# A third PSUM bank for the ring of turns and projections, taken from the score maxima

## The reference

```
# block 1: attention with a modulated norm, no mask
xn   = rms_norm(x, g_norm) * (1 + scale(cond)) + shift(cond)
q,k,v = split(xn @ W_qkv);  q = rms_norm(q, g_q); k = rms_norm(k, g_k)   # per head
a    = softmax(q k^T / sqrt(32)) v
x1   = a + a @ W_out

# block 2: attention with a latent, rotary halves and a causal mask, then experts
n    = rmsnorm(x1, ln1)
kv_d, q_d = n @ kv_d_w, n @ q_d_w                     # 128 wide
k = [kv_d @ k_u_w | rope(n @ rope_k_w)];  q = [q_d @ q_u_w | rope(q_d @ rope_q_w)]
v = kv_d @ v_u_w
h = x1 + softmax(causal(q k^T / sqrt(32))) v @ o_w
m = rmsnorm(h, ln2)
out = x + h + expert_shared(m) + sum over the top 2 of 7 routed experts(m)
```

## Time and profile before

| | |
|---|---|
| median of 3 runs | 1290.48 us |
| the profiled execution | 1290.86 us |
| its span, first to last instruction | 1289.1 us |
| TensorE busy | 1169.7 us (91%) |
| VectorE busy | 744.4 us (58%) |
| ScalarE busy | 572.3 us (44%) |
| GpSimd busy | 290.7 us (23%) |
| mean granted TensorE clock | 0.97 of full speed |
| chain that ended last, by engine | PE 77%, DVE 8%, DMA 5%, ACT 4% |

### The profile page before, as it was taken

One profiled execution on the slowest core, in us unless ns is written; L12 is line 12 of the kernel. 1 busy time (PEld: TensorE's weight loads), 2 busy tenths in 40 slices (PEclk: granted clock), 3 DMA queues, 4 the chain that ended last, 5 costly groups with the idle time before them and its releaser, 6 DMA issues.

```text
span 1289.1 us, 18670 instructions
## 1 busy us (share of the span) xinstructions
PE 1169.7 (91%) x6059; PEld 825.7 (64%) x6059; DVE 744.4 (58%) x1807; ACT 572.3 (44%) x1248; POOL 290.7 (23%) x244
## 2 busy tenths in 40 slices
PE   5979999999999889999999989989999999999970
PEld 5745555665566446557767757766657888888850
DVE  6565675477545856666565575566364774444433
ACT  3324464345443555455465454455264753222210
POOL 1313122100210031001011200200124464555530
PEclk9979999999999999999999999999899999999995
DMA  7064243125311732352284264265357744555559
GB/s 255 33 180 131 65 136 112 50 86 184 99 50 58 225 107 57 99 189 88 88 259 149 86 234 122 84 201 176 86 186 232 262 152 105 109 108 113 115 134 331
DMA packets 88127, 178.42 MB, mean 138 GB/s; under 512 B 12609, under 2 KB 23265, under 8 KB 86497
## 3 DMA queue, kind: packets, MB, share of 16 engines
q1 hardware_dynamic: 79216, 156.90, 37.4%
q0 software_dynamic: 8512, 19.93, 8.2%
q10 hardware_dynamic: 304, 0.40, 0.2%
HBM read 110.86 MB, written 65.27 MB: 137 GB/s over the span
## 4 chain that ended last, share of the span: by engine, by line
PE 77%; DVE 8%; DMA 5%; ACT 4%; issue 3%; SPq 1%; POOL 0%; DVEq 0%; ACTq 0%; POOLq 0%
PE psum L862 14%; PE psum L681 9%; PE psum L682 8%; PE psum L683 8%; PE psum L846 6%; PE psum L825 6%; PE psum L690 4%; PE psum L940 4%; PE psum L942 4%; PE psum L941 4%; PE psum L967 2%; PE psum L969 2%; PE psum L968 2%; PE psum L909 2%; PE psum L772 2%
## 5 line engine op out<-in xcount | busy, mean ns | idle before, releaser
L1174 ACT ACTIVATE probs<-psum 128x512 f32<-128x512 f32 (+3 forms) x512 | 257.3, 517 | 231.5 <-PE psum L849 120.6
L825 PE MATMUL psum<-stack 96*128 96x512 f32 (+3 forms) x512 | 210.2, 416 | 8.6 <-DMA stack<-split_s 4.0
L1583 DVE TENSOR_REDUCE nmax<-psum 128x1 f32<-128x512 f32 x256 | 170.5, 684 | 77.0 <-PE psum L825 73.2
L846 PE MATMUL psum<-stack 97*128 97x512 f32 (+3 forms) x512 | 197.3, 386 | 16.8 <-ACT probs L1174 15.4
L862 PE MATMUL psum<-probs,vals 128*33 128x512 f32 (+3 forms) x1024 | 209.4, 531 | 0.0
L1586 DVE CUSTOM_DVE_ANT_0 psum<-psum,causal 128x128 f32<-128x128 f32 (+3 forms) x256 | 123.0, 501 | 21.0 <-PE psum L825 19.4
L825 PEld LDWEIGHTS psum<-stack 96*128 96x128 f32 x512 | 100.0, 196 | 46.3 <-issue 23.7
L846 PEld LDWEIGHTS psum<-stack 97*128 97x128 f32 x512 | 99.0, 193 | 40.0 <-ACT probs L1174 25.8
L862 PEld LDWEIGHTS psum<-probs,vals 128*33 128x33 f32 x1024 | 49.8, 112 | 99.6 <-issue 65.5
L681 PE MATMUL psum<-w_hi,xh 128*128 128x512 f32 (+1 forms) x256 | 95.4, 373 | 4.2 <-DVEq L1449 2.5
L682 PE MATMUL psum<-w_hi,xl 128*128 128x512 f32 (+1 forms) x256 | 93.6, 366 | 0.0
(11 more groups left out here) (238 smaller groups left out, 2338.0 us busy)
## 6 DMA issues: line engine op xcount, KB each, us to landing
stack<-split_s SPq DMA_DIRECT2D x378, 128.0 KB, 3.0
split_s<-split SPq DMA_DIRECT2D x64, 512.0 KB, 3.0
xt<-in_x_dram SPq DMA_DIRECT2D x4, 1024.0 KB, 5.2
x_s<-yt SPq DMA_DIRECT2D x4, 1024.0 KB, 5.0
xt<-x_s SPq DMA_DIRECT2D x4, 1024.0 KB, 4.8
yt<-in_x_dram SPq DMA_DIRECT2D x4, 1024.0 KB, 5.6
res<-x_s SPq DMA_DIRECT2D x4, 1024.0 KB, 8.2
acc_s<-yt SPq DMA_DIRECT2D x4, 1024.0 KB, 6.0
```

Source lines behind the costliest of these rows:

```text
L825: sq.filled(nc.tensor.matmul(psum[:, sq.bank(M), 0:n], st[:, 0, t * P:(t + 1) * P], st[:, 1, 0:n], start=True, stop=True), M)
L846: last = nc.tensor.matmul(psum[:, bank, lo:S], st[:, 1, t * P:(t + 1) * P], st[:, 0, lo:S], start=True, stop=not masked)
L1174: sk.cleared(nc.scalar.activation(probs[:, M % NX, lo:S], psum[:, sk.bank(M), lo:S], ACT.Exp, scale=SCALE), M)
L1583: sq.cleared(V.tensor_reduce(out, psum[:, sq.bank(M), :], AX.X, ALU.max, negate=True), M)
```

## The change

The ring of turns and projections gets the banks 0, 1 and 6, the scores keep 2 and 3. Its items are numbered anew at the end: from the list AFTER on (the last pieces beside the experts), a number that would fall on bank 6 is passed over, so that these pieces use banks 0 and 1 as before. The first use of bank 6 by the experts waits for the last item of the ring in it, not for the last score. Three places that freed a bank with a fixed `% 2` now take the ring's length. The order of the instructions is the same on all five engines; what differs is for which earlier instruction TensorE waits, and the bank.

```
+RING_BANKS = (0, 1, 6)
+
+def two_banks_at_end(numbers):
+    n = min(numbers[key] for key in AFTER if key in numbers)
+    for key in AFTER:
+        if key in numbers:
+            n += n % len(RING_BANKS) == 2
+            numbers[key] = n
+            n += 1
+    return numbers
+
+RING_NO = two_banks_at_end(RING_NO)
+LAST_IN_6 = max((key for key in RING_NO if RING_NO[key] % len(RING_BANKS) == 2), key=RING_NO.get)
...
-        ring = Ring("ring", sem, (0, 1), RING_NO)
-        sq = Ring("scores", sem, (2, 3, 6))
+        ring = Ring("ring", sem, RING_BANKS, RING_NO)
+        sq = Ring("scores", sem, (2, 3))
...
                 elif i == 0:
-                    sq.wait_read(pe, NSTEPS - 3)
+                    ring.wait_read(pe, LAST_IN_6)
...
-                dve.sem_inc(ring.free[RING_NO[key] % 2], 1)
+                dve.sem_inc(ring.free[RING_NO[key] % ring.n], 1)
```

## The result

| | before | after |
|---|---|---|
| median, us (runs) | 1291.38 (1288.5 to 1295.52, 4) | 1304.14 (1304.07 to 1309.36, 4) |
| the profiled execution, us | 1290.86 | 1304.21 |
| its span, us | 1289.1 | 1302.4 |
| ratio of the times | | 1.0088, 95% interval 1.0053 to 1.0124 |

The kernel became slower, by 11.4 us going by the ratio, by 13.3 us going by the two spans. I had forecast 23.5 us. So the sign held, and so did the place and the cause of the cost; the size was about twice too large. Lines 690 to 862 of before are 706 to 878 of after, 16 further down.

A forecast was written before the change was run, and what follows sets the result against it. TensorE was taken as the engine whose gaps count, 54.5 us of them in the heads. Score cost 41.3 less ring gain 15.2 less 2.6 where both meet gives +23.5 us on 1290.86: 1314 us, 8-in-10 range 1296 to 1332.

The forecast's parts named there:

- Direction, places, names: Heads: slower; score waits for nmax grow from 2.7 to some 30 to 50 us, ring waits nearly vanish, TensorE's work stays.
- the likeliest case: Whole kernel: the prediction's own forecast of 1314 us, range 1300 to 1327 us, chance 0.62.
- Term 1: TensorE's waits for the ring in the heads: a third bank gains 15.2 us, 6.2 before 433 us and 9.0 behind.
- The gross waits: Ring in the heads: 52 late starts, together 34.4 us, taken as the upper end of the third bank's gain.
- Term 2: Scores in the heads: two banks make them wait for maxima, costing 41.3 us, 10.7 before 433 us and 30.6 behind.
- The gross lateness: Scores from step 24 on: largest lateness of each of 60 late runs, summed to 55.5 us, before taking off existing waits.
- The first steps: Earliest scores, up to step 21: VectorE already sets the pace, so a bank less changes nothing.
- Term 3: Six late score runs behind turned x tiles: the third ring bank fills these sooner, taking 2.6 us off the cost.
- The start and the experts: Start up to 76 us and experts keep their length; the 4.24 us ring wait there is worth nothing.
- One lag, two names: VectorE's queue, heads: moving a bank only renames the wait, no change, 1291 us; chance 0.13, at 1287 to 1297.
- Slower by more: Heads: nothing absorbed (+40 us, 1331 us), and the clock may add; chance 0.16, at 1323 to 1340 us.
- The ring was the shortage: Heads: delayed scores cost only 10 us, the ring gains 25 of 34.4, so faster, around 1276 us; chance 0.09.

The follow-up runs named there:

- e1: The kernel before with the scores on two banks and the ring still on two, bank 6 unused until the experts; 1317.02 us, ratio 1.0193.
- e4: The kernel before with 232 extra score products, overwritten afterwards, placed in 58 of the late runs by their lateness; 1313.82 us, ratio 1.0152.
- e9: e8 with bank 6 left to the scores for the steps up to 16, then given to the ring; 1282.19 us, ratio 0.9922 to before.
- e8: The kernel after with VectorE's maxima one step earlier in its queue from step 176 on; 1283.55 us, ratio 0.9931 to before.
- e5: The kernel before with 232 extra score products, overwritten afterwards, spread at even distances; 1317.57 us, ratio 1.0197.
- e7: The kernel after with 24 extra products into an unused bank in one place ahead of the heads; 1304.55 us, ratio 1.0077 to before.
- e6: The kernel before with 22 extra products into an unused bank ahead of the heads; 1291.78 us, ratio 0.999.

## Why the prediction was right, and why its size was not

**Direction, places, names.** Right. The score's waits appear all through the heads (77 in the two rows of nmax) and more in block 2, the ring's nearly vanish, TensorE's work stays. The time, 1304.1 us, lies in the range given, and in the likeliest case's own range of 1300 to 1327, near its lower end. Some of that is luck: the cost was put 15.7 us too high and the gain (15.2 + 2.6) 4.9 us too high, and the two errors partly cancel.

**Term 1, the ring: 15.2 us.** Measured 12.9 by e1 against after, 11.7 by their spans. Behind step 192 the same stretches show 8.9 us (-0.6 + 5.5 + 4.0) for the forecast 9.0; of the 6.2 before it only 2.7 are there (-0.7 + 3.4). With stretches that repeat within 2.5 us only, the 8.9 fits better than it had to. The gross waits of 34.4 us would have been far off. The method, follow each wait to the next score and keep only what its maximum allows, held; the places of the earlier trace rows came out nearly as worked out.

**Term 2, the scores: 41.3 us.** Measured 25.6. This is the step that failed in size. The gross lateness, 55.5 us, is borne out: idle time before the scores' weight loads grew in e1 by 58.2 us (46.3 to 104.5). What failed is "taking off, run by run, the waits that TensorE has there anyway". I took off only waits that ended before the needed maximum did, 14.2 us. The delays also used up waits that came later: before the transposed scores' loads the idle time fell from 40.0 us to 17.2 in e1, and the wait itself from 15.4 to 1.7, where I had expected a third less. The reason I gave, that VectorE is idle 39% of the time and so "a delay then carries over whole", is wrong, as e4 shows directly: of 40.7 us more of busy time 23.1 arrived. Where TensorE would wait for an exponential anyway, a delay ahead of that place is taken back at it; e4 shows it by its row of exponentials, 15.4 to 2.7 us.

By stretch: up to step 192, at 433 us, the forecast was 10.7 us and e1 cost 3.3 (3.2 + 0.1); in steps 32 to 192 11.7 us of new waits met 8.7 us of old ones that went. Behind step 192 it was 30.6 against 21.2: 13.6 us in steps 192 to 320 (21.5 of new waits, 8.3 of old ones gone; 1.7 of it is half clock) and 7.6 behind step 320. There the clock has a part: e1 stands at half clock for 13.6 us less than before, worth 6.8. Over all the heads the clock gives e1 3.7 us (31.2 us at half clock for 38.6) of the 16.3 us by which its span is below my cost; the other 12.6 are cover that I left out. The six executions of e1 bear the 3.7 out: against before at the same clock the cost is 29 us, 3.6 more than the 25.6.

**The first steps.** That "a bank less changes nothing" there was wrong: it cost 3.2 us in e1, 3.9 in after. I had read that VectorE sets the pace and overlooked that it does so only while a third bank lets TensorE work ahead. e9, which leaves the bank there, loses 1.2 us in these steps and e8 4.0.

**Term 3, -2.6 us.** Not measured by itself; it is inside the 12.9 us, which then has to be set against 15.2 + 2.6 = 17.8. Whether it exists stays open.

**The start and the experts.** Same length, to 0.5 us. The ring wait of 4.24 us before the heads is gone, and the first score starts at 76.46 us as before 76.48: the stack's transfer hid it, as forecast.

**The rivals.** *One lag, two names* falls: the third bank of the ring by itself is worth 12.9 us. *Slower by more* falls: about half of the delays were absorbed, and the half clock of the heads went from 38.6 to 36.6 us although the gaps grew from 54.5 to 64.4. In e1, with still more gaps, the mean clock is higher than before, not lower. *The ring was the shortage* was half right in its reason, absorption by the exponentials' waits; it failed by its numbers, 10 us of cost and 25 of gain against 25.6 and 12.9. The Trainium skill, Perfetto Trace Analysis, section Optimization Strategy, says that a repeating gap can mean too little PSUM for the next tile. In this case's trace the repeating gaps it points to did nearly vanish with a third bank (26.6 to 5.0 us), and were worth 12.9 us, not the 34.4 that I had put to that rule.

**What stays open.** How much of the 11.6 us that e5 loses in steps 32 to 192, where e4 loses nothing, is the even spacing: e5 has 35 products more there, 8 us. And why the clock falls where it does. After has 10.2 us more at half clock than before in steps 192 to 320, some 5 of its 14.2 us. That isn't one execution's chance alone: e7, with the same banks, has the same 13.7 us there, its falls at the same times within 0.5 us, and the same +14.1. But e6, with the banks of before, also has 10.2 us at half clock there and is only 1.5 us longer, so the half clock is the smaller part of the 14.2 us.

## What to carry to other kernels

When a PSUM bank goes from one ring to another, count for both rings how late each item would be, not the waits that the table shows: the ring that doesn't wait with three banks may be the one that can't do with two. Then take off waits behind a delay too, up to the next late one, not only those that end before it: here between a third and a half of some 50 us of delays was covered, at the late places and, somewhat less, at even distances, on a TensorE that is 91% busy. Which bank split wins depends on the order in the reader's queue, and on the part of the program: compare kernels stretch by stretch at the same steps and join the better parts, as e8 did with two orders that were slower than before each. Look at the mean clock beside every time: a difference of 0.004 was worth 5 us here, as much as half of what e8 gained.

## What was not expected of the hardware

The 22 products of e6 didn't keep off the fall of the clock at the start. TensorE was busy for 5.79 us of 66 to 72 us and 4.70 of 72 to 78 (4.07 and 2.60 in before); then it stood idle 1.45 us, and the fall came at 79.5 instead of 74.1 us. It lasted 13.7 us instead of 17.1, but all stretches at half clock from the first score to the last were 44.4 us in e6 and 38.6 in before. The times of the two agree (ratio 0.999).
